# Transposes of 4-byte data written as products with the identity, in 32-column tiles

## What is computed

```
h = relu(patches @ W.T + b); batch-normalise h over all positions
n = layernorm(h)
q, k, v = n @ Wq.T + bq, n @ Wk.T + bk, n @ Wv.T + bv        # 8 heads of 16
h = h + merge(softmax(q @ k.T / 4) @ v) @ Wo.T + bo
n = layernorm(h); e = argmax(n @ Wr + br)                    # 8 experts, one is chosen
h = h + relu(n @ W1[e] + b1[e]) @ W2[e] + b2[e]
```

## Time and profile before

| | us |
|---|---|
| runs | 1410.22 median of 3 (1408.41 to 1411.82) |
| profiled execution, its own time | 1411.15 |
| its span | 1409.1 |
| PE busy | 1259.2 (89%), 21768 instructions |
| DVE busy | 1093.6 (78%) |
| ACT busy | 968.1 (69%) |
| POOL busy | 594.4 (42%) |

### The profile page before, as it was taken

How to read it: one execution, slowest core, us unless ns; L and a number is a source line. 1 busy time by engine, 2 the same in 40 slices (tenths; PEclk the granted TensorE clock), 3 DMA queues, 4 the chain that set the end, 5 groups by cost and what they waited for, 6 DMA issues and landing times.

```text
span 1409.1 us, 54650 instructions
## 1 busy us (share of the span) xinstructions
PE 1259.2 (89%) x21768; PEld 780.5 (55%) x21768; DVE 1093.6 (78%) x3006; ACT 968.1 (69%) x2479; POOL 594.4 (42%) x544
## 2 busy tenths in 40 slices
PE   6377999999999999999999999999999862999996
PEld 3123546454555555555555455555555431989996
DVE  8368898888888888888888888888889313667775
ACT  5212878787878778787878787877767850667774
POOL 1122424343444536353434344453621222556664
PEclk9558999999999999999999999999999985999999
DMA  7145041423325050404142232505040502333331
GB/s 174 42 57 100 19 84 43 83 66 60 78 48 104 21 120 21 107 36 90 48 78 69 57 82 44 110 15 121 21 107 3 159 24 68 94 88 103 106 104 51
DMA packets 70383, 102.51 MB, mean 73 GB/s; under 512 B 14828, under 2 KB 59875, under 8 KB 69710
## 3 DMA queue, kind: packets, MB, share of 16 engines
q1 hardware_dynamic: 60992, 78.68, 25.2%
q0 software_dynamic: 8416, 20.22, 5.1%
q10 hardware_dynamic: 762, 0.55, 0.1%
HBM read 60.96 MB, written 39.00 MB: 71 GB/s over the span
## 4 chain that ended last, share of the span: by engine, by line
PE 63%; DVE 14%; ACT 11%; issue 5%; DMA 4%; POOL 2%; SPq 1%; another core or an unknown queue 0%; POOLq 0%; ACTq 0%; DVEq 0%
PE psum L977 30%; PE psum L1052 11%; DVE half_max L850 10%; PE psum L982 7%; PE psum L1106 6%; PE psum L1116 6%; ACT arena L605 5%; DMA arena<-in_x_t_dram 2%; ACT q_full L593 1%; ACT k_full L593 1%; DMA k_rows<-k_parts_dram 1%; SPq L399 1%; ACT k_part L593 1%; PE psum L996 1%; PE psum L1097 1%
## 5 line engine op out<-in xcount | busy, mean ns | idle before, releaser
L850 DVE TENSOR_REDUCE half_max<-psum 128x1 f32<-128x373 f32 x1536 | 773.6, 538 | 143.3 <-PE psum L977 134.4
L605 ACT ACTIVATE arena<-psum 128x373 f32<-128x373 f32 (+1 forms) x1536 | 667.3, 487 | 248.6 <-PE psum L977 241.6
L977 PE MATMUL psum<-k_rows,arena 96*32 96x373 bf16 x6144 | 525.5, 332 | 27.4 <-DMA k_rows<-k_parts_dram 15.5
L977 PE MATMUL psum<-arena,k_rows 98*32 98x373 bf16 x6144 | 513.1, 325 | 12.6 <-ACT arena L605 11.6
L1052 PE MATMUL psum<-arena,values 128*32 128x373 f32 (+1 forms) x3072 | 314.0, 476 | 1.5 <-ACT arena L605 1.2
L977 PEld LDWEIGHTS psum<-k_rows,arena 96*32 96x32 bf16 x6144 | 180.2, 97 | 182.6 <-DVE half_max L850 90.4
L977 PEld LDWEIGHTS psum<-arena,k_rows 98*32 98x32 bf16 x6144 | 177.8, 95 | 158.4 <-ACT arena L605 67.5
L503 POOL DMA_INDIRECT routed_rows_dram<-rows,pos_i x96 | 96.2, 1002 | 338.2 <-DVE tok_id L844 247.1
L543 POOL DMA_INDIRECT out_dram<-arena,slot_id x102 | 122.8, 1204 | 88.0 <-issue 52.1
L1052 PEld LDWEIGHTS psum<-arena,values 128*32 128x32 f32 (+1 forms) x3072 | 99.9, 110 | 27.4 <-issue 1.9
L527 POOL TENSOR_TENSOR rstd<-var_eps,minus_half 128x6 f32<-128x6 f32 x16 | 21.5, 1347 | 203.1 <-DVE var_eps L727 203.1
(11 more groups left out here) (155 smaller groups left out, 1442.5 us busy)
## 6 DMA issues: line engine op xcount, KB each, us to landing
arena<-q_parts_dram SPq DMA_DIRECT2D x192, 93.2 KB
k_rows<-k_parts_dram SPq DMA_DIRECT2D x192, 93.2 KB
arena<-routed_rows_dram SPq DMA_DIRECT2D x102, 130.0 KB
q_parts_dram<-q_part SPq DMA_DIRECT2D x16, 559.5 KB, 3.2
k_parts_dram<-k_part SPq DMA_DIRECT2D x16, 559.5 KB, 3.2
arena<-in_x_t_dram SPq DMA_DIRECT2D x3, 703.1 KB, 17.6
seq<-in_w_dram SPq DMA_DIRECT2D x1, 2048.0 KB, 10.3
seq<-in_w_dram SPq DMA_DIRECT2D x8, 256.0 KB, 5.8
```

The lines of the kernel that those rows point to most:

```text
L605: nc.scalar.activation(probs[0:kn(kt), G % N_P, j, :], st_bank[s % N_ST][0:kn(kt), 0:HALF], ACT.Exp).then_inc(s_exp, 1)
L850: nc.vector.tensor_reduce(half_max[:, s:s + 1], mx_bank[s % N_MX][:, 0:HALF], AX.X, ALU.max)\
L977: last = nc.tensor.matmul(dst[n:n + m], weights[:, n:n + m], moving, start=start, stop=stop)
```

## The change

In the helper `transposes` each of the three blocks is now made by `quad`, with the block as weights and the identity as the moving operand. Instead of one 128-column transpose (L982) a block is four products (L977), each of which loads 32 columns of the block and writes 32 rows of `misc`. The blocks of `misc` hold the same data in the same places. A fill holds twelve products where it held three transposes. The order of the fills, their steps, their waits and the lists of the other engines are as before. The 2-byte transposes and those behind the bodies are not touched.

```
             def transposes(part, src):
                 for n in range(3):
-                    last = nc.tensor.transpose(misc[:, D * n:D * (n + 1)], src(3 * part + n), ident[:, :])
+                    last = quad(misc[:, D * n:D * (n + 1)], src(3 * part + n), ident[:, :])
                 return last
```

## The result

| | before | changed |
|---|---|---|
| median of 4 runs each, same chip | 1411.02 us (1408.41 to 1412.29) | 1445.29 us (1441.26 to 1447.95) |
| ratio, 95% interval | | 1.0242 (1.0221 to 1.0264) |
| profiled execution / its span | 1411.15 / 1409.1 us | 1447.95 / 1446.2 us |

The change costs 34.3 us where the forecast had 25.6: 1445.3 against 1435.8, inside the range of 1423 to 1446 and outside the likeliest case's own range of 1431 to 1441. The question is where 8.7 us more came from.

The account below looks back on a forecast made before the run. PE was taken to pace the middle, with serial stretches at half clock. Unwaited fills 6.7, waited 10.1, last attention body 0.9, serial 7.3 and ramp 0.6 made +25.6 us on 1410.22: 1435.8 us, range 1423 to 1446.

Parts of the forecast that it names:

- the likeliest case: Whole kernel: the forecast sum of +25.6 us, 1435.8 us, with its own range 1431 to 1441; chance 0.70.
- rival C: Unwaited fills: the 0.10 us gap before a fill stays, so each costs 0.18 us; 1447.0 us, chance 0.10.
- What bounds the kernel: Middle, 130 to 1103 us: paced by PE, busy 924.34 of 973 us, with DVE not far behind.
- The price of an unwaited fill: Fills PE reaches without waiting: 0.66 against 0.58 us, gap gone, +0.08 us each; 84 counted, 6.7 us.
- The price of a waited fill: Fills PE waits for: removing the gap gives nothing, +0.18 us each; 56 in the middle, 10.1 us.
- The wait itself stays as it is: Waited fills in the middle: PE's wait keeps its length, as ACT and DVE are shifted with PE.
- The cover of the OT0 fills: Steps 11 and 15 of a body: DVE is slower there, so 28 fills cost nothing; uncovered, 2.2 us.
- It moves nothing, adds no wait: Whole kernel: the edit only swaps transposes for products in each fill and changes no other engine's list.
- Serial stretch and ramp: Outside the middle: 12 serial fills at clock 0.50, +0.61 us each, 7.3 us; four ramp fills, 0.6 us.
- A: Serial stretches: products raise the clock to its full grant, 12.2 us less than forecast, 1423.6 us; chance 0.08.
- B: Middle: DVE's or ACT's backlog swallows 0.08 us of each of 84 unwaited fills; 1429.1 us, chance 0.09.
- D: Fills: a product block costs only a transpose's step, 0.42 us a fill, no gap; 16.8 us faster, 1393.4 us; chance 0.03.

Follow-up runs that it names:

- e10: Changed kernel with POOL's six scatters released at steps 0, 4, 8, 12, 17, 22 instead of 0, 3, 6, 9, 12, 15; 1430.86 us.
- e11: Kernel before with POOL's six scatters released at steps 0, 4, 8, 12, 17, 22 instead of 0, 3, 6, 9, 12, 15; 1400.86 us.
- e12: Kernel before with only the last body's eight fills, in the serial stretch, made as products; 1413.84 us, ratio 1.0033.
- e4: Changed kernel with each block made as one product of 128 columns instead of four of 32; 1477.41 us, ratio 1.0474.
- e8: Changed kernel with each block made as two products of 64 columns instead of four of 32; 1471.43 us, ratio 1.0446.
- e3: Kernel before, transposes kept, with twelve 8-column products into unread columns of misc added to each fill; 1460.88 us, ratio 1.0363.
- e5: Kernel before with only HTOK and OT0 fills as products, and each body's first row loads held until score product 24; 1422.09 us, ratio 1.0102.
- e7: Changed kernel with each body's first group of row loads held until score product 24; 1442.91 us, ratio 1.0244.

## Why the prediction was right, and where it was short

The direction, the engine that paces the kernel and most of the prices were right. That the time lies inside the range is in part luck: the room above 1441 us was there for rival C, which is refuted.

- **What bounds the kernel**: right. PE paces the middle in all these kernels, and an addition to PE's list is paid nearly in full.
- **The price of an unwaited fill, +0.08 us, with the gap gone**: right for the `o_un` fills (0.16, then 0.66). The fill from `arena` takes 0.68 and 0.02 in front, +0.12, and steps 18 to 72 with eight fills cost 1.00 us for 0.94. I had one measured row, PROJ's, and took it for all.
- **The price of a waited fill, +0.18 us**: measured +0.20 to 0.21. "The wait itself stays as it is" was right: 7.6, 3.1 and 2.8 us in after for the three releasers, 7.6, 3.2 and 3.0 in the earlier trace rows.
- **The cover of the OT0 fills**: borne out for the first of them in the bodies with scatters (-0.06 us at steps 10 to 14). At the second it can't be told from the halts (+0.21 together).
- **"It moves nothing, adds no wait"**: here the sum is short. The edit was read for semaphores and durations alone. A later PE meets POOL's scatters at another moment, and the exponential behind the second HTOK fill, on time in most bodies before, is late in nearly all: +0.41 us a body, which the sum doesn't have. And each fill holds twelve instructions for three: where two scatters come back to back PE's list halts, "issue" 8.9 us in the middle instead of 0.6. Most of that falls into time in which the kernel before waits for ACT, so its net size is +0.21 us a body.
- **The sum of the miss in the middle**, 10.9 us in the profiled executions: 13 x 0.41 = 5.3 at steps 6 to 10, 13 x 0.21 = 2.7 at steps 14 to 18, 13 x 0.06 = 0.8 for prices, 13 x 0.14 = 1.8 behind step 72, which I can't explain, and -0.8 at steps 10 to 14; the remaining 1.1 isn't broken down. By e10 and e11, with the scatters spread, the change costs 0.66 us a body less (0.44 without the odd body of e11), and 34.3 - 30.0 = 4.3 us less by medians. So about half of the 8.7 us that the medians are off hangs on the old places of the scatters; the other 4.4 stays with the spread ones and isn't placed; 13 x 0.36 = 4.7 would be its size by e11's usual bodies (1.56 against the forecast 1.2).
- **Serial stretch and ramp**: 12 x 0.61 right in the row (1.51 us), +5.6 instead of +4.9 for the eight fills after the last body in the profiled execution; e12 gives 4.8. Prologue and ramp 1.8 of 3.0.
- **Rivals**: A refuted (clock 0.50). B refuted (the body grew by 2.00, not under 0.7). C's 1447.0 lay nearest to the time, for a reason that was not the cause: the gap is gone, and a body grew by more than the 1.7 us that I had named as C's mark. A mark on a sum alone can't tell two causes apart; the rows of single fills did. D refuted (a fill takes 0.66, above the 0.58 from which it decides). The Trainium skill's factor of four for FP32 ("TensorE: Matmul & The Clock Gate", section "Terms") would have made a fill an estimated 1.92 us; the rows have 0.66 and 0.68 against 0.48, a factor of 1.4.

**What stays open.** How a scatter on POOL holds up ACT's next exponential or PE's next instruction. Shown is that PE's halts need both: with 6 and 12 records a fill (e4, e8) or with spread scatters (e10) one to three short ones are left of 28, and in body 1, without scatters, they are absent; with transposes but as many instructions more (e3) they are there; and they aren't tied to the row loads (e5, e7). Shown is also that the late exponentials go with the scatters' places (e10, e11). That the queue of the instruction lists and the scatters' own traffic meet is a guess; no run changed the scatters' traffic or held that queue apart. Why one late start falls on the exponential of step 8 in the changed kernel and mostly not in the kernel before is argued from the moment alone.

## What to carry to other kernels

A transpose of 4-byte blocks as four 32-column products is paid for here by 0.66 to 0.68 us against 0.48 per three blocks, of which the neighbours' equal tile width gives back 0.10; no fill of this kernel gains by it. When an edit multiplies an engine's instructions, count them, and look for groups of one instruction's tiles broken in the middle and for "issue" in the waits. But don't take the total of such a row for its price: compare the starts of one instruction a step in both kernels, which shows where time is lost and what was lost there already. Where GpSimd's indirect scatters run beside a full engine, give each its distance: one tuple was worth 8 us to the kernel before and 12 to 14 to the changed one (1445.29 or 34.3 us above before as it was, 1430.86 or 21.8 with the scatters spread).

## What the runs showed of the hardware

- A change of tile width, 32 to 128 or 32 to 64 columns, costs 0.10 to 0.11 us before the first instruction at the new width, for transposes and products alike; from 32 to 32 columns it is nothing, 4-byte data included.
- Three 128x128 blocks of 4-byte data take 0.48 us as transposes, 0.66 to 0.68 as products in 32-column tiles, 0.81 in 64-column tiles (gap apart), 0.86 as whole products.
- Beside two scatters 1.3 us apart PE halts for 0.3 to 0.4 us at a time, twice a body, in the middle of a group of four, for nothing that the profile shows, and also with a body's row loads moved away (e7).
- Beside the scatters ACT starts an exponential late though its product is done: 1.55 us after the product's start in before and 1.73 in after at step 16, against 0.45 without scatters (body 1) or with spread ones (e10, e11).
- TensorE kept a granted clock of 0.50 (1.2 GHz) for 25 us in which it was busy 13.2 us, nearly all of it with products (7.05 of 10 us at the densest, 1190 to 1200).
